# Expert layers of a fused network: gathered rows transposed two tiles ahead, result stores three tiles behind the loads of weight pieces

## The chip, the cores and the metric

The kernel runs as one program on one NeuronCore of a Trainium2 chip. Its time is the device time of one execution in microseconds; the figure compared is the median of several executions. Engines: TensorE (PE in the profile, with PEld for its weight loads), VectorE (DVE), ScalarE (ACT), GpSimd (POOL), SyncE (SP), and 16 DMA engines. All five work through their own instruction streams in order, and meet at semaphores.

## What is computed

The network has four layers: an adaptive convolution with a box convolution, a softmax attention with a mixture of experts, and a linear attention with a second mixture of experts. The change touches the two mixtures of experts alone. Of 4096 tokens of 128 channels each, every one goes to its 2 best of 8 experts:

```python
g = jnp.einsum('sd,edh->esh', flat, w_gate)
u = jnp.einsum('sd,edh->esh', flat, w_up)
y = jnp.einsum('esh,ehd->esd', silu(g) * u, w_down)
out = jnp.einsum('esd,se->sd', y, dense_w)      # dense_w: softmax over the two chosen
```

The hidden width is 256 in the first expert layer (names with `d_`) and 512 in the second (names with `f_`).

## The kernel before

Routing sorts the (token, expert) pairs into 71 tiles of 128 rows, each tile with one expert. `experts` is then called once for each layer, and goes over these 71 tiles. The order on each engine is written out by hand, and semaphores join the engines. For tile n:

- **GpSimd** gathers the tile's 128 rows from HBM into one of four buffers `xg` by an indirect DMA (`gather`), AHEAD = 3 tiles in front of its own loop; gather n waits until tile n-4 has been transposed. In the second layer it also writes the results by an indirect DMA (`scatter`).
- **TensorE** transposes the rows into PSUM (`transpose_x`), forms gate and up in three passes (`gate_up`: high x high, high x low, low x high parts of numbers split in two), transposes the hidden tile (`transpose_h`) and multiplies it by the expert's output weights (`down`). Before `transpose_x` it reads the number of the expert into a register (`load_expert`, a TENSOR_LOAD).
- **ScalarE** applies Silu to gate (`gate`), copies the transposed rows to SBUF as the high part (`copy_x`), and copies the transposed hidden tile (`copy_h`).
- **VectorE** subtracts to get the low part (`low_x`), multiplies up by Silu(gate) (`hidden`), and copies the result out of PSUM (`result`).
- **SyncE**, in the first layer, stores the result tile to HBM.

TensorE's loop body is the part that the change is about: `gate_up(n)`, `transpose_x(n+1)`, `transpose_h(n-1)`, `down(n-2)`. `gate_up(n+1)` waits for `low_x(n+1)`, which waits for `copy_x(n+1)`, which stands behind `gate(n)` on ScalarE, which waits for `gate_up(n)`.

The first layer also prepares the input weights of the second, in 16 pieces of 128x512 (256 KB), one in each of its first 16 tiles (`WeightSplit`, names `f_raw`, `f_w_high`, `f_w_low`). SyncE loads a piece into one of two buffers, ScalarE copies it as the high part at the end of its loop body (L1181), and VectorE subtracts for the low part at the end of its own (L1190). The load of piece n+2 waits for the low part of piece n. On SyncE it stands between the stores of result n-1 and n; result n-1 is made two loop bodies after its gate_up.

PSUM: in the first layer the transposed rows and the results have two banks each; in the second one each (`OWN = 1`), so that `transpose_x(n)` there waits for `low_x(n-1)`. The SBUF tiles of high and low parts have two buffers each in both layers.

Of the kernel before, what the change touches and what calls it, by code (L numbers as in the profile page):

```python
# [27 lines left out]
P = 128  # L28
# [34 lines left out]
class Kit:  # L63
# [7 lines left out]
    def sb(self, name, shape, dt=F32):  # L71
        return self.ctx.enter_context(self.nc.sbuf_tensor(name, shape, dt))

    def sem(self, name):
        s = self.ctx.enter_context(self.nc.semaphore(name))
        Kit.used.append(s)
        return s
# [1674 lines left out]
def experts(nc, top, moe, split=None):  # L1752
# [4 lines left out]
    ps, ident = top.ps, top.ident  # L1757
    F, TILES_IN = moe.F, moe.SLOT_TILES
    CHUNKS = F // P
    AHEAD = 3  # L1760
    RING = 8
    tag = moe.tag
    with ExitStack() as ctx:  # L1763
# [9 lines left out]
        y = sb("y", [P, RING, C])  # L1773
        gathered = sem(*(f"gathered{b}" for b in range(4)))
        stored = sem(*(f"stored{b}" for b in range(RING)))
        xT_ps, x_high_ready, x_ready, gu_ps, silu_ready, h_ready, h_ps, hT_ready, y_ps, y_ready = sem(
            "xT_ps", "x_high_rd", "x_rd", "gu_ps", "silu_rd", "h_rd", "h_ps", "hT_rd", "y_ps", "y_rd")
# [12 lines left out]
        if moe.by_slot:  # L1790
            @block.sync
            def _(sp):
                if split is not None:
                    for i in range(2):
                        split.load(sp, i)
                for n in range(TILES_IN):
                    if split is not None and n + 2 < split.pieces:
                        split.load(sp, n + 2)
                    sp.wait_ge(y_ready, n + 1)
                    sp.dma_start(moe.y_dram[n * P:(n + 1) * P, :], y[:, n % RING]).then_inc(stored[n % RING], 16)  # L1800
                for b in range(RING):
                    sp.wait_ge(stored[b], 16 * ((TILES_IN - b + RING - 1) // RING))

        @block.gpsimd
        def _(pool):
# [13 lines left out]

            for n in range(AHEAD):  # L1820
                gather(n)
            for n in range(TILES_IN):
                if n + AHEAD < TILES_IN:
                    gather(n + AHEAD)
                if not moe.by_slot and n >= 3:
# [7 lines left out]
        @block.tensor  # L1833
        def _(pe):
            keep_warm(nc, top, 3, 7)
            pe.wait_ge(moe.weights_in, 16)
            expert = [pe.alloc_register(f"{tag}_expert{b}") for b in range(4)]

            nc.disable_value_cache = True

            def of_expert(w, n):
                e = bass.RuntimeValue.of_register_unchecked(expert[n % 4]).with_bounds(min_val=0, max_val=moe.E - 1)
                return w[:, bass.ds(e, 1), :].rearrange("p e f -> p (e f)")

            def load_expert(n):
                pe.reg_load(expert[n % 4], moe.expert[0:1, n:n + 1])

            def transpose_x(n):
                pe.wait_ge(gathered[n % 4], 16 * (n // 4 + 1))
                if n >= OWN:  # L1850
                    pe.wait_ge(x_ready, n - OWN + 1)
                nc.tensor.transpose(XT(n), xg[:, n % 4, :], ident[:]).then_inc(xT_ps, 1)  # L1852

            def gate_up(n):
                pe.wait_ge(x_ready, n + 1)
                if n >= 2:
                    pe.wait_ge(h_ready, n - 1)
                passes = ((xT, moe.w_high), (xT, moe.w_low), (xT_low, moe.w_high))
                for i, (x, w) in enumerate(passes):
                    if wide:  # L1860
                        for o, cols in ((GATE(n), slice(0, F)), (UP(n), slice(F, 2 * F))):
                            ins = nc.tensor.matmul(o, x[:, n % 2, :], of_expert(w, n)[:, cols],  # L1862
                                                   start=(i == 0), stop=(i == len(passes) - 1))
                    else:
                        ins = nc.tensor.matmul(ps[:, n % 2, 0:2 * F], x[:, n % 2, :], of_expert(w, n),  # L1865
                                               start=(i == 0), stop=(i == len(passes) - 1))
                ins.then_inc(gu_ps, 1)

            def transpose_h(n):
                pe.wait_ge(h_ready, n + 1)  # L1870
                if n >= 2:
                    pe.wait_ge(hT_ready, n - 1)
                for c in range(CHUNKS):
                    ins = nc.tensor.transpose(HT(n)[:, c * P:(c + 1) * P], h[:, n % 2, c * P:(c + 1) * P], ident[:])
                ins.then_inc(h_ps, 1)

            def down(n):
                pe.wait_ge(hT_ready, n + 1)
                if n >= OWN:
                    pe.wait_ge(y_ready, n - OWN + 1)  # L1880
                for c in range(CHUNKS):
                    e = bass.RuntimeValue.of_register_unchecked(expert[n % 4]).with_bounds(min_val=0, max_val=moe.E - 1)
                    ins = nc.tensor.matmul(Y(n), hT[:, n % 2, c * P:(c + 1) * P],  # L1883
                                           moe.w_out[:, bass.ds(e, 1), c, :].rearrange("p e c -> p (e c)"),
                                           start=(c == 0), stop=(c == CHUNKS - 1))
                ins.then_inc(y_ps, 1)

            load_expert(0)
            transpose_x(0)
            for n in range(TILES_IN + 2):  # L1890
                if n < TILES_IN:
                    gate_up(n)
                if n + 1 < TILES_IN:
                    load_expert(n + 1)
                    transpose_x(n + 1)
                if 1 <= n <= TILES_IN:
                    transpose_h(n - 1)
                if n >= 2:
                    down(n - 2)
            nc.disable_value_cache = False  # L1900

        @block.scalar
        def _(act):
            def gate(n):
                act.wait_ge(gu_ps, n + 1)
                if n >= 2:
                    act.wait_ge(h_ready, n - 1)
                nc.scalar.activation(silu[:, n % 2, :], GATE(n), ACT.Silu).then_inc(silu_ready, 1)  # L1908

            def copy_x(n):  # L1910
                act.wait_ge(xT_ps, n + 1)
                if n >= 2:
                    act.wait_ge(gu_ps, n - 1)
                nc.scalar.activation(xT[:, n % 2, :], XT(n), ACT.Copy).then_inc(x_high_ready, 1)  # L1914

            def copy_h(n):
                act.wait_ge(h_ps, n + 1)
                if n >= 2:
                    act.wait_ge(y_ps, n - 1)
                nc.scalar.activation(hT[:, n % 2, :], HT(n), ACT.Copy).then_inc(hT_ready, 1)  # L1920

            copy_x(0)
            for n in range(TILES_IN + 1):
                if n < TILES_IN:
                    gate(n)
                if n + 1 < TILES_IN:
                    copy_x(n + 1)
                if n >= 1:
                    copy_h(n - 1)
                if split is not None and n < split.pieces:  # L1930
                    split.high_on_scalar(act, n)

        @block.vector
        def _(dve):
            def low_x(n):
                dve.wait_ge(x_high_ready, n + 1)
                nc.vector.tensor_tensor(xT_low[:, n % 2, :], XT(n), xT[:, n % 2, :], ALU.subtract).then_inc(x_ready, 1)  # L1937

            def hidden(n):
                dve.wait_ge(silu_ready, n + 1)  # L1940
                if n >= 2:
                    dve.wait_ge(h_ps, n - 1)
                nc.vector.tensor_tensor(h[:, n % 2, :], UP(n), silu[:, n % 2, :], ALU.mult).then_inc(h_ready, 1)  # L1943

            def result(n):
                dve.wait_ge(y_ps, n + 1)
                if n >= RING:
                    dve.wait_ge(stored[n % RING], 16 * (n // RING))
                nc.vector.tensor_copy(y[:, n % RING, :], Y(n)).then_inc(y_ready, 1)  # L1949

            low_x(0)
            for n in range(TILES_IN + 2):
                if n + 1 < TILES_IN:
                    low_x(n + 1)
                if n < TILES_IN:
                    hidden(n)
                if n >= 2:
                    result(n - 2)
                if split is not None and n < split.pieces:
                    split.low(dve, nc.vector, n)  # L1960
# [187 lines left out]
```

## Time and profile before

| | us |
|---|---|
| median of 3 executions | 969.69 (969.58 to 978.5) |
| the profiled execution | 975.88 |
| its span, first to last instruction | 974.1 |
| mean granted clock of TensorE | 0.871 of full speed |
| first expert layer's tiles, in the span | about 394 to 551 |
| second expert layer's tiles, in the span | about 729 to 943 |

Times of day below are microseconds from the start of the span. The granted clock is 1.00 at 2.4 GHz and 0.50 at 1.2 GHz. In the profile a matmul's duration includes the way through the array, so matmuls that follow each other overlap: the distance from start to start is what one costs. Float32 matmuls of `down` appear as two records each.

### The profile page before, as it was taken

The page shows a single profiled execution, that of the slowest core. Times are in us where ns is not written, and L with a number is a line of the kernel's source. Part 1 is how long each engine was busy: PE and PEld are TensorE (multiplying, and loading weights), DVE is VectorE, ACT ScalarE, POOL GpSimd, SP SyncE. Part 2 cuts the span into 40 slices and gives each one's busy share as a digit, 9 for nine tenths or more (in the row PEclk, how much of TensorE's full clock was granted, in tenths as well). Part 3 has the DMA queues.
Part 4 walks back from the last instruction along what each step waited for, and adds up shares of the span by engine and source line. Part 5 has one row for each costly group of instructions (what it writes and reads, how often), then busy time and mean ns, then how long its engine had stood idle before and what let it go on. Part 6 is the DMA issues. An engine that isn't in the chain of part 4 may idle for free. (4 is left out here: it accounts for less than half of the span.)

```text
span 974.1 us, 17847 instructions
## 1 busy us (share of the span) xinstructions
PE 746.4 (77%) x4853; PEld 590.5 (61%) x4853; DVE 544.4 (56%) x1589; ACT 456.9 (47%) x1147; POOL 437.2 (45%) x464
## 2 busy tenths in 40 slices
PE   3797978989998736769999535566479999999960
PEld 1575846666665535446666424554367888888850
DVE  6587946777775559354444255776573333333326
ACT  1994435767775314444444334552144444444424
POOL 5000444655652060434444277831015666666734
PEclk9899887999997755899999867987559999999995
DMA  2000000000000240452222211102201111111107
GB/s 97 1 0 19 3 1 2 2 0 0 0 1 2 77 140 1 119 147 64 66 66 66 54 49 50 49 16 76 98 8 34 44 44 47 42 47 41 50 19 259
DMA packets 34197, 46.24 MB, mean 47 GB/s; under 512 B 8227, under 2 KB 22887, under 8 KB 33872
## 3 DMA queue, kind: packets, MB, share of 16 engines
q1 hardware_dynamic: 25264, 27.66, 8.8%
q0 software_dynamic: 8864, 17.72, 6.9%
q8 instruction: 36, 0.59, 0.3%
q14 instruction: 33, 0.27, 0.1%
HBM read 30.21 MB, written 15.60 MB: 47 GB/s over the span
## 5 line engine op out<-in xcount | busy, mean ns | idle before, releaser
L1809 POOL DMA_INDIRECT d_xg<-d_normed,d_gather x71 | 68.3, 961 | 104.5 <-PE ps L1852 79.6
L1047 DVE TENSOR_REDUCE negmax<-ps 128x2 f32<-128x512 f32 x128 | 82.6, 688 | 51.9 <-PE ps L881 51.1
L1809 POOL DMA_INDIRECT f_xg<-f_normed,f_gather x71 | 69.0, 971 | 78.5 <-SPq L1763 55.0
L1908 ACT ACTIVATE f_silu<-ps 128x512 f32<-128x512 f32 x71 | 42.5, 598 | 118.9 <-PE ps L1862 118.9
L1937 DVE TENSOR_TENSOR f_x_low<-ps,f_x_high 128x128 fp32r<-128x128 f32 x71 | 20.7, 292 | 135.5 <-ACT f_x_high L1914 135.5
L1815 POOL DMA_INDIRECT f_results<-f_y,f_scatter x71 | 71.9, 1013 | 54.4 <-issue 39.3
L788 ACT ACTIVATE prob<-ps 128x512 f32<-128x512 f32 x128 | 69.6, 598 | 44.4 <-PE ps L900 44.4
L1261 POOL DMA_INDIRECT e_yg<-d_results,d_slot_u x64 | 61.0, 953 | 32.9 <-issue 18.2
L1883 PE MATMUL ps<-f_w_out,f_hT 128*128 x568 | 75.2, 275 | 0.7 <-DVE f_y L1949 0.7
L1883 PEld LDWEIGHTS ps<-f_w_out,f_hT 128*128 128x128 f32 x568 | 69.0, 192 | 0.9 <-issue 0.9
L1937 DVE TENSOR_TENSOR d_x_low<-ps,d_x_high 128x128 fp32r<-128x128 f32 x71 | 20.6, 290 | 73.6 <-ACT d_x_high L1914 73.6
L1908 ACT ACTIVATE d_silu<-ps 128x256 f32<-128x256 f32 x71 | 27.1, 382 | 67.5 <-PE ps L1865 67.5
L725 POOL TENSOR_SCALAR q_low<-q,lower 128x512 fp32r<-128x512 f32 x16 | 24.9, 1559 | 66.3 <-ACT q L768 45.5
L1865 PE MATMUL ps<-d_w_high,d_x_high 128*128 x71 | 35.7, 503 | 23.9 <-DVE d_x_low L1937 15.8
L1862 PE MATMUL ps<-f_w_high,f_x_high 128*128 x142 | 51.7, 445 | 2.7 <-DVE f_x_low L1937 2.7
L898 PE MATMUL ps<-qa,ka 32*128 32x256 f32 x256 | 42.7, 348 | 11.8 <-DVE qb L1053 8.9
L1345 PE MATMUL ps<-ident,e_xn 128*128 128x128 f32 x32 | 9.0, 374 | 55.0 <-ACT e_xn L1311 55.0
L1943 DVE TENSOR_TENSOR f_h<-ps,f_silu 128x512 f32<-128x512 f32 x71 | 48.3, 681 | 1.8 <-ACT f_silu L1908 1.7
L1883 PE MATMUL ps<-d_w_out,d_hT 128*128 x284 | 48.2, 292 | 0.1
L327 PE MATMUL ps<-fcol,wimg 128*128 (+1 forms) x160 | 41.0, 404 | 5.9 <-ACT wimg L283 5.5
L1862 PE MATMUL ps<-f_w_high,f_x_low 128*128 x142 | 44.8, 396 | 0.0
L1862 PE MATMUL ps<-f_w_low,f_x_high 128*128 x142 | 44.6, 395 | 0.0
(353 smaller groups left out, 2105.0 us busy)
## 6 DMA issues: line engine op xcount, KB each, us to landing
d_results<-d_y SPq DMA_DIRECT2D x71, 64.0 KB
f_raw<-in_f_in SPq DMA_DIRECT2D x16, 256.0 KB, 2.8
f_ys<-f_results SPq DMA_DIRECT2D x8, 512.0 KB, 7.3
X<-in_x SPq DMA_DIRECT2D x4, 512.0 KB, 5.5
d_normed<-X SPq DMA_DIRECT2D x8, 256.0 KB, 2.0
d_raw<-in_d_in SPq DMA_DIRECT2D x8, 256.0 KB, 2.8
f_normed<-X SPq DMA_DIRECT2D x8, 256.0 KB, 2.0
f_w_out<-in_f_out SPq DMA_DIRECT2D x1, 2048.0 KB, 8.2
```

Source lines behind the costliest of these rows:

```text
L327: last = nc.tensor.matmul(ps[:, 2 + b, a * PIX:(a + 1) * PIX], wimg[:, a, t, :], rhs.rearrange("p n r c -> p (n r) c"), start=(t == 0), st ...
L788: nc.scalar.activation(prob[:, h].rearrange("p t q -> p (t q)"), ps[:, h % 2, :], ACT.Exp, scale=SCALE).then_inc(prob_ready, 1)
L898: nc.tensor.matmul(o, ka[rows, b, g, keys], qa[rows, b, g, :], start=True, stop=False)
L1047: nc.vector.tensor_reduce(negmax[:, :, h // HG, col:col + 1], ps[:, 2 + h % 2, :].rearrange("p (t k) -> p t k", t=2), AX_X, ALU.max, negat ...
L1261: nc.gpsimd.indirect_dma_start(yg[:, n % 4, t, c, :], None, first.y_dram, bass.IndirectOffsetOnAxis(ap=first.slot[:, c, tile:tile + 1], ax ...
L1809: nc.gpsimd.indirect_dma_start(xg[:, n % 4, :], None, moe.xn_dram, bass.IndirectOffsetOnAxis(ap=moe.gather[:, n:n + 1], axis=0)).then_inc( ...
L1815: nc.gpsimd.indirect_dma_start(moe.y_dram, bass.IndirectOffsetOnAxis(ap=moe.scatter[:, n:n + 1], axis=0), y[:, n % RING, :], None, bounds_ ...
L1862: ins = nc.tensor.matmul(o, x[:, n % 2, :], of_expert(w, n)[:, cols], start=(i == 0), stop=(i == len(passes) - 1))
L1883: ins = nc.tensor.matmul(Y(n), hT[:, n % 2, c * P:(c + 1) * P], moe.w_out[:, bass.ds(e, 1), c, :].rearrange("p e c -> p (e c)"), start=(c ...
L1908: nc.scalar.activation(silu[:, n % 2, :], GATE(n), ACT.Silu).then_inc(silu_ready, 1)
L1937: nc.vector.tensor_tensor(xT_low[:, n % 2, :], XT(n), xT[:, n % 2, :], ALU.subtract).then_inc(x_ready, 1)
L1943: nc.vector.tensor_tensor(h[:, n % 2, :], UP(n), silu[:, n % 2, :], ALU.mult).then_inc(h_ready, 1)
```

## The change

Three orders are changed in `experts`, for both layers, and one on SyncE, for the first:

- `transpose_x`, `copy_x` and `low_x` run for tile n+2 where they ran for n+1. Two of each stand ahead of the loops. On VectorE `low_x` moves behind `hidden`.
- Gathers run 4 tiles ahead (AHEAD) instead of 3, still in four buffers.
- SyncE stores result n-3 in loop body n instead of result n; the loads of weight pieces keep their bodies.

```diff
-    AHEAD = 3
+    AHEAD = 4
...
-                for n in range(TILES_IN):
+
+                def store(n):
+                    sp.wait_ge(y_ready, n + 1)
+                    sp.dma_start(moe.y_dram[n * P:(n + 1) * P, :], y[:, n % RING]).then_inc(stored[n % RING], 16)
+
+                for n in range(TILES_IN + 3):
                     if split is not None and n + 2 < split.pieces:
                         split.load(sp, n + 2)
-                    sp.wait_ge(y_ready, n + 1)
-                    sp.dma_start(moe.y_dram[n * P:(n + 1) * P, :], y[:, n % RING]).then_inc(stored[n % RING], 16)
+                    if n >= 3:
+                        store(n - 3)
...
             load_expert(0)
-            transpose_x(0)
+            for n in range(2):
+                transpose_x(n)
             for n in range(TILES_IN + 2):
                 if n < TILES_IN:
                     gate_up(n)
                 if n + 1 < TILES_IN:
                     load_expert(n + 1)
-                    transpose_x(n + 1)
+                if n + 2 < TILES_IN:
+                    transpose_x(n + 2)
                 if 1 <= n <= TILES_IN:
                     transpose_h(n - 1)
                 if n >= 2:
...
-            copy_x(0)
+            for n in range(2):
+                copy_x(n)
             for n in range(TILES_IN + 1):
                 if n < TILES_IN:
                     gate(n)
-                if n + 1 < TILES_IN:
-                    copy_x(n + 1)
+                if n + 2 < TILES_IN:
+                    copy_x(n + 2)
...
-            low_x(0)
+            for n in range(2):
+                low_x(n)
             for n in range(TILES_IN + 2):
-                if n + 1 < TILES_IN:
-                    low_x(n + 1)
                 if n < TILES_IN:
                     hidden(n)
+                if n + 2 < TILES_IN:
+                    low_x(n + 2)
                 if n >= 2:
                     result(n - 2)
```

SyncE's stream at the start of the first expert layer, as a difference (- before, + after); f_raw is a weight piece, d_results a result tile:

```order
-L1177 DMA f_raw<-in_f_in 128x512 x3
-L1800 DMA d_results<-d_y 128x128
+L1177 DMA f_raw<-in_f_in 128x512 x6
+L1799 DMA d_results<-d_y 128x128
```

Six loads now stand ahead of the first store, where three did; each later load stands three stores further ahead.

VectorE's stream at the same place, before: d_x_low is `low_x`, d_h is `hidden`, f_w_low the low part of a weight piece.

```order
L1937 TENSOR_TENSOR d_x_low<-ps,d_x_high 128x128 x2
L1943 TENSOR_TENSOR d_h<-ps,d_silu 128x256
L1190 TENSOR_TENSOR f_w_low<-f_raw,f_w_high 128x512
L1937 TENSOR_TENSOR d_x_low<-ps,d_x_high 128x128
L1943 TENSOR_TENSOR d_h<-ps,d_silu 128x256
```

The same place after:

```order
L1945 TENSOR_TENSOR d_x_low<-ps,d_x_high 128x128 x2
L1951 TENSOR_TENSOR d_h<-ps,d_silu 128x256
L1945 TENSOR_TENSOR d_x_low<-ps,d_x_high 128x128
L1190 TENSOR_TENSOR f_w_low<-f_raw,f_w_high 128x512
L1951 TENSOR_TENSOR d_h<-ps,d_silu 128x256
```

The two ahead are now both in front of the loop, and each later `low_x` stands behind `hidden` of the same body.

ScalarE's first rows of the layer, before: d_x_high is `copy_x`, and the table load is that of Silu.

```order
L1914 ACTIVATE d_x_high<-ps 128x128
L1908 ACT_TABLE_LOAD
L1908 ACTIVATE d_silu<-ps 128x256
L1914 ACTIVATE d_x_high<-ps 128x128
L1181 ACTIVATE f_w_high<-f_raw 128x512
```

The same rows after:

```order
L1921 ACTIVATE d_x_high<-ps 128x128 x2
L1915 ACT_TABLE_LOAD
L1915 ACTIVATE d_silu<-ps 128x256
L1921 ACTIVATE d_x_high<-ps 128x128
L1181 ACTIVATE f_w_high<-f_raw 128x512
```

The table load and the first Silu now stand behind the copy of the second tile. Further on the streams read alike, one tile apart in what their rows work on.

## Rows read from the trace of the kernel before

**Rows 1.** Windows: each engine's busy us (x instructions), clock, DMA share, GB/s.

```profile
395.50:440.00 44.50, 30.92 (x160) 22.68 (x160) 22.99 (x64) 23.10 (x67) 17.38 (x18) 0.96 0.47 131
440.00:547.00 107.00, 97.43 (x531) 71.67 (x531) 43.64 (x160) 44.02 (x159) 46.70 (x50) 1.00 0.25 65
742.00:937.00 195.00, 195.00 (x1264) 174.33 (x1263) 72.86 (x201) 83.39 (x200) 129.41 (x131) 1.00 0.16 44
```

**Rows 2.** Waits in 386 to 552 us: who waited for whom, total us, times, longest.

```profile
ACT d_silu L1908 <- PE ps L1865: 67.5, 58, 1.5
```

**Rows 3.** Timeline of one first-layer tile: start us, us, engine, line, op, [idle before].

```profile
492.43 0.50 PE L1865 MATMUL ps<-d_w_high,d_x_high 128*128 x1
...
493.43 0.38 ACT L1908 ACTIVATE d_silu<-ps 128x256 f32<-128x256 f32 x1 [1.19 <-PE ps L1865]
...
493.60 0.69 PE L1883 MATMUL ps<-d_w_out,d_hT 128*128 x4
493.71 0.27 ACT L1914 ACTIVATE d_x_high<-ps 128x128 fp32r<-128x128 f32 x1
...
494.01 0.29 DVE L1937 TENSOR_TENSOR d_x_low<-ps,d_x_high 128x128 fp32r<-128x128 f32 x1 [1.20 <-ACT d_x_high L1914]
...
494.45 0.49 PE L1865 MATMUL ps<-d_w_high,d_x_high 128*128 x1 [0.16 <-issue]
```

**Rows 4.** Timeline of one second-layer tile.

```profile
802.74 0.27 PE L1852 MATMUL ps<-ident,f_xg 128*128 128x128 f32 x1
...
802.93 0.60 ACT L1908 ACTIVATE f_silu<-ps 128x512 f32<-128x512 f32 x1 [1.69 <-PE ps L1862]
...
803.28 1.06 PE L1883 MATMUL ps<-f_w_out,f_hT 128*128 x8
...
803.94 0.68 DVE L1943 TENSOR_TENSOR f_h<-ps,f_silu 128x512 f32<-128x512 f32 x1
...
804.17 0.73 PE L1862 MATMUL ps<-f_w_high,f_x_high 128*128 x2
...
805.67 0.27 PE L1852 MATMUL ps<-ident,f_xg 128*128 128x128 f32 x1
```

**Rows 5.** L1809, gathers of both layers: from issue to landing.

```profile
DMA to landing us min/median/max: 2.5/2.6/3.8
```

**Rows 6.** Timeline around one weight piece, from the store ahead to its use.

```profile
402.98 0.33 SPq L1800 DMA_DIRECT2D d_results<-d_y  x1
...
403.35 0.43 SPq L1177 DMA_DIRECT2D f_raw<-in_f_in  x1
...
406.11 0.63 ACT L1181 ACTIVATE f_w_high<-f_raw 128x512 fp32r<-128x512 f32 x1 [1.72 <-DMA f_raw<-in_f_in]
...
406.77 0.69 DVE L1190 TENSOR_TENSOR f_w_low<-f_raw,f_w_high 128x512 fp32r<-128x512 f32 x1 [1.80 <-ACT f_w_high L1181]
```

**Rows 7.** The tile f_raw, the raw weight pieces.

```profile
L1181 ACT ACTIVATE f_w_high<-f_raw x16: 622/630/642, 396.9 to 438.3; 128x512 fp32r<-128x512 f32 x16
...
DMA to landing us min/median/max: 2.7/2.8/3.1
```

**Rows 8.** Timeline of ScalarE where the weight pieces end.

```profile
438.87 0.39 ACT L1908 ACTIVATE d_silu<-ps 128x256 f32<-128x256 f32 x1
...
441.02 0.38 ACT L1908 ACTIVATE d_silu<-ps 128x256 f32<-128x256 f32 x1 [1.33 <-PE ps L1865]
```

**Rows 9.** Timeline of the first layer's start.

```profile
391.61 0.95 POOL L1809 DMA_INDIRECT d_xg<-d_normed,d_gather  x1 [0.30 <-issue]
...
395.05 1.28 ACT L1908 ACT_TABLE_LOAD   x1
...
396.51 0.38 ACT L1908 ACTIVATE d_silu<-ps 128x256 f32<-128x256 f32 x1 [0.17 <-PE ps L1865]
```

**Rows 10.** Timeline of TensorE at the second layer's start.

```profile
733.75 0.72 PE L1862 MATMUL ps<-f_w_high,f_x_high 128*128 x2 [1.16 <-DVE f_x_low L1937]
...
736.67 0.74 PE L1862 MATMUL ps<-f_w_high,f_x_high 128*128 x2 [0.72 <-DVE f_x_low L1937]
```

## The prediction

> **What bounds the kernel now.** I looked first at windows over the two places that the change touches. In the second expert layer TensorE is busy 195.00 of 195 us at clock 1.00; in the first it is busy 97.43 of 107 us once the weight pieces are done, and only 30.92 of 44.5 us while they last [rows 1]. So the second layer is bound by TensorE itself and can give back only what its start loses; the first has room. The waits of the first layer say why: ScalarE waited 67.5 us for gate_up before Silu, in 58 of 71 tiles [rows 2].
>
> The timeline of one tile shows the circle [rows 3]. gate_up starts at 492.43; Silu starts at 493.43, when it is done; the copy of the next tile's rows stands behind Silu, at 493.71; low_x follows at 494.01 and ends at 494.30; only then does the next gate_up start, at 494.45. That is 2.02 us a tile, though TensorE's fourth down matmul began about 0.4 us after 493.60 and nothing follows it. low_x(n+1) depends on transpose_x(n+1) alone by its data; only ScalarE's order ties it to gate_up(n).
>
> **Part 1: transposes two ahead, first layer, tiles after the weight pieces.** After the change gate_up(n+1) needs low_x(n+1) of one body earlier, ready about 2 us before it is asked for. The circle is then Silu, copy, low_x once in two tiles: 2.02 / 2 = 1.0 us a tile, and no longer the bound. What is late next? TensorE's own work. From gate_up's start to the first down matmul it is 1.17, over three gate_up passes and three transposes [rows 3]. Four down records cost 4 x 0.11 = 0.45 at the second layer's pace (0.89 us for eight, 803.28 to 804.17 [rows 4]), or about 0.55 as they stand in the first (0.69 for four, less the last one's 0.29, makes 0.13 to 0.14 between starts). So 1.62 to 1.72 a tile. A second way: 9.57 us idle over 53 tiles is 0.18 each [rows 1], and each gap hides behind a modelled matmul end of 0.29 where the next start could have come after 0.13: 0.18 + 0.16 = 0.34 to be had, 1.68. I take 1.66, in the middle.
>
> The others keep up with 1.66. ScalarE's three operations start 0.28, then 0.16 apart, and the last takes 0.39: 0.83. VectorE's three are of similar size, about 0.8. A gather is 0.95 plus 0.30 of issue, 1.25 [rows 9], and takes 2.6 us to land, 3.8 at worst [rows 5]. Its place: AHEAD grows with the transposes, so gather n still starts when transpose_x(n-4) is done and has four tiles, 6.6 us, before transpose_x(n) asks for it, which queues transpose_h and down behind it on TensorE. 0.3 + 3.8 = 4.1 fits into 6.6. Had AHEAD stayed 3 GpSimd would not wait for longer either, since nothing but gathers stands in its stream here. The stores move behind by three tiles, which ring buffer y (8) covers: VectorE's result(n) needs store n-8.
>
> Sum: 52 tiles (18 to 70) x (2.02 - 1.66) = **18.7 us**; with 1.72 it is 15.6, with 1.60 it is 21.8.
>
> **Part 2: the 16 tiles with weight pieces.** Now the load at 403.35 stands behind the store at 402.98, which waited for result 0, though its buffer had been free for two microseconds; the piece reaches ScalarE at 406.11, where the copy had waited 1.72 us and all of ScalarE's next body with it [rows 6]. High parts run from 396.9 to 438.3 in 15 steps, 2.76 us a tile [rows 7]. With the stores three behind, the result that a store waits for is always there (result n-3 is made in body n-1, low part n in body n), so a load waits only for the low part of the piece in its buffer. What is late next is that circle itself: high part to low part 0.66, low part 0.69, issue about 0.04, landing 2.76 here [rows 6] and 2.7 to 3.1 over all [rows 7]; with 2.9 it is 4.29 us for the two tiles between uses of a buffer, **2.15 a tile** instead of 2.76. This is above TensorE's 1.66 and above ScalarE's 0.83 + 0.63 = 1.46, so the loads stay the bound here, and part 1 alone would give nothing on top.
>
> The start costs something. copy_x(1) now stands ahead of Silu's table load (1.28 us), and needs the second gather, issued at 391.61 [rows 9]. With 3.7 to land (near the worst of [rows 5]) it arrives at 395.3, the copy is done at about 396.0, the table at 397.3: Silu(0) at 397.3 instead of 396.51 [rows 9], 0.8 later, and with it piece 0. If the gather lands in 2.6 this cost is gone. Then: low part 0 done at 399.1, piece 2 at ScalarE at 402.0, six turns of 4.29 to piece 14 at 427.7, piece 15 about 1.3 behind at 429.0, against 438.3. Silu(16) comes at 429.6 instead of 438.87, 9.3 us sooner. Before, Silu(17) came at 441.02 [rows 8] and Silu(18) one tile of 2.02 later, 443.04. After, TensorE has had both gate_ups ready or free to start, and Silu(18) comes at about 431.5: **11.5 us** saved up to there. With landings of 3.1 it is 10; with 2.7 and no loss at the start it is 13.5.
>
> The DMA engines are 0.47 busy at 131 GB/s while the pieces load [rows 1]. A piece and two row tiles in 2.15 us are 384 KB, about 183 GB/s, or 0.66 busy at the same price: room, but less of it. The Trainium skill ("DMA: Bandwidth & Descriptors", Latency and other measured facts) gives HBM's access latency as 0.2 us on average and 2 us at high load, which would speak against a landing as short as today's. By it a landing could grow by up to 1.8 us and the circle to 3.0 a tile, slower than before in this stretch by 4 us; no row here shows such a landing.
>
> **Part 3: the second layer.** TensorE starts a transpose of rows every 2.93 us (802.74, 805.67 [rows 4]), and its work is the same, so nothing changes in steady state. One bank holds the transposed rows here, so transpose_x(n+2) waits for low_x(n+1), which VectorE now makes behind hidden(n-1). Silu starts at 802.93, 1.70 after its gate_up (804.17 less 2.93); with Silu 0.60, hidden 0.68 [rows 4], low_x 0.29 as in the first layer and 0.1 of handing over, low_x ends 3.4 after gate_up(n-1), 0.5 after gate_up(n), and the transpose is asked for 1.5 after it: 1.0 us of slack. At the start TensorE waited 1.16 us before gate_up(1) and 0.72 before gate_up(2) [rows 10]; these 1.9 go. The table load behind copy_x(1), and transpose_x(1) waiting for low_x(0) ahead of gate_up(0), cost 0.2 to 0.4. Net **1.5 us**. The ends of both layers are as they were, and what follows moves with them.
>
> **Sum.** 18.7 + 11.5 + 1.5 = 31.7 us. The profiled execution of 975.88 would become 944.2. It is 6.2 us above the median of 969.69; I take the saving off the median as it is: **938 us**, 3.3% less.
>
> **Rivals.**
> 1. *TensorE's instruction supply sets the tile.* Each first-layer tile has a TENSOR_LOAD and five address instructions among its matmuls. If they run only at the pace seen after a release, a tile is 1.17 + 0.55, and 0.15 from the releasing low_x (494.30) to gate_up (494.45): 1.87 [rows 3]. Part 1 shrinks to 52 x 0.15 = 7.8, and the time is 949. For it: down starts 0.13 apart here against 0.11 there. Against: the second layer runs without a gap with ten address instructions and a TENSOR_LOAD in 2.93 us [rows 1, 4]. The Trainium skill ("DMA: Bandwidth & Descriptors", Latency and other measured facts) puts the floor of a tensor_load at about 600 ns, which speaks for this rival: by it one load a tile would leave 1.06 of 1.66 us for the other instructions. No row shows the register read by itself.
> 2. *The loads gain nothing*, because stores and gathers lengthen landings by as much as the queue loses: 2.76 a tile stays. Part 2 shrinks to the two tiles behind the pieces, about 2: 947.5. Against: landings were 2.7 to 3.1 with a store right ahead of each load.
> 3. *Steady tiles stay at 2.02*, because the new order closes another circle that I don't see: the wait moves and the time is 957. Against: no circle over two tiles that I can draw is longer than 1.46 a tile beside TensorE's.
> 4. *Slower: the single bank of the second layer.* If low_x(n+1) behind hidden(n-1) comes late, transpose_h and down queue behind a waiting transpose. Each 0.1 us past the 1.0 of slack costs 7.1 us over 71 tiles; from 0.45 us late, thus low_x 1.45 us later than I reckon, the change is a loss, and at 0.6 the time is 981. Silu and hidden would have to start far later than they do.
>
> **How the numbers follow.** Forecast 0.62 (own range 932 to 944); rival 1 0.14; rival 2 0.07; rival 3 0.06; rival 4 0.03; more gain than forecast, if tiles reach 1.55, 0.05; nothing gained at all 0.03. The range is 930 to 949.5. A measurement of this kernel can tell about 1% from no change. Faster by over 1% (below 960): 0.93. Within 1%: 0.04. Slower: 0.03.
>
> **What would show it.** In the profile after: Silu of the first layer 1.6 to 1.7 us apart behind the pieces, TensorE without idle time there, and ScalarE's 67.5 us of waits for gate_up still long but harmless; loads issued within 0.1 us of the low part and high parts 2.15 apart in pairs; the second layer's tiles still 2.93 apart. Wrong would be: waits of TensorE for gathers, landings well over 3.1, or a gap before each transpose of the second layer.

## The result: 4.8 to 5.6% faster, more than forecast

| | before | after | ratio, 95% interval |
|---|---|---|---|
| first measurement, median | 969.63 us (4 executions) | 917.47 us (4) | 0.9438 [0.9374, 0.9503] |
| measured again, median | 971.97 us (11) | 925.88 us (6) | 0.9525 [0.9488, 0.9562] |
| profiled execution, its span | 974.1 us | 918.5 us | |

Medians are over all executions; ratios and their intervals leave out those that took over 1.5% longer than the fastest of the same kernel.

The forecast was 938 us, in a range of 930 to 949.5. The time is below it. The profiles say where, in stretches between events that both traces have (first gather of the first layer, weight load of the linear attention, first gather of the second layer, load of the results for the last sum):

| stretch, us | before | before, second trace | after | after, second trace |
|---|---|---|---|---|
| up to the first expert layer | 390.1 | 380.4 | 381.5 | 384.8 |
| first expert layer | 162.8 | 162.4 | 125.2 | 125.3 |
| linear attention and routing | 173.2 | 172.1 | 171.8 | 172.9 |
| second expert layer | 224.1 | 225.3 | 216.3 | 215.0 |
| last sum | 23.9 | 23.9 | 23.7 | 23.8 |

The expert layers gave 37 and 8 to 10 us, 45 to 47 together. The stretch ahead of them, which nobody edited, takes 380 to 390 us; that is the likely reason why the first measurement shows 52 us.

The windows of the kernel after, behind the weight pieces and in the second layer, with the same columns as in [rows 1]; the first stretch is that with the pieces:

```profile
388.00:421.00 33.00, 27.16 (x158) 20.04 (x157) 21.75 (x61) 21.33 (x64) 17.06 (x18) 1.00 0.62 174
424.00:498.00 74.00, 74.00 (x498) 64.00 (x496) 40.44 (x148) 41.37 (x150) 44.33 (x47) 1.00 0.35 88
695.00:880.00 185.00, 185.00 (x1242) 164.48 (x1241) 71.55 (x195) 81.60 (x196) 126.71 (x128) 1.00 0.16 46
```

TensorE now shows 74.00 of 74 us in the first layer as well, where it showed 97.43 of 107 [rows 1]. The waits in the first layer, against [rows 2]:

```profile
ACT d_silu L1915 <- PE ps L1870: 35.5, 53, 0.8
...
ACT f_w_high L1181 <- DMA f_raw<-in_f_in: 11.7, 14, 1.8
...
PE ps L1879 <- DVE d_h L1951: 6.0, 11, 1.2
```

ScalarE waits for gate_up 35.5 us instead of 67.5, and behind the pieces this wait is now harmless: TensorE has no idle time there. TensorE waits 6.0 us for `hidden` in 11 waits, in tiles with pieces and at the end, since it shows no idle time from 424 to 498.

One tile of the first layer, as in [rows 3]:

```profile
442.40 0.48 PE L1870 MATMUL ps<-d_w_high,d_x_high 128*128 x1
...
442.67 0.28 DVE L1945 TENSOR_TENSOR d_x_low<-ps,d_x_high 128x128 fp32r<-128x128 f32 x1
...
443.39 0.38 ACT L1915 ACTIVATE d_silu<-ps 128x256 f32<-128x256 f32 x1 [0.65 <-PE ps L1870]
...
443.51 0.61 PE L1888 MATMUL ps<-d_w_out,d_hT 128*128 x4
...
443.88 0.48 PE L1870 MATMUL ps<-d_w_high,d_x_high 128*128 x1
```

A tile takes 1.48 us (442.40 to 443.88) instead of 2.02. `low_x` at 442.67 is for the next gate_up, at 443.88. It ends at 442.95, 0.93 before that gate_up starts, where the prediction reckoned with about 2 and the kernel before had 0.14 to 0.15.

One tile of the second layer, as in [rows 4]:

```profile
800.44 0.27 PE L1857 MATMUL ps<-ident,f_xg 128*128 128x128 f32 x1
...
800.99 1.06 PE L1888 MATMUL ps<-f_w_out,f_hT 128*128 x8
801.80 0.72 PE L1867 MATMUL ps<-f_w_high,f_x_high 128*128 x2
...
803.27 0.27 PE L1857 MATMUL ps<-ident,f_xg 128*128 128x128 f32 x1
```

A transpose of rows comes every 2.83 us (800.44 to 803.27) instead of every 2.93. Most of the tenth went ahead of gate_up: from the first down matmul to gate_up it is 0.81 (800.99 to 801.80), and it was 0.89 (803.28 to 804.17 [rows 4]).

The tile f_raw, as in [rows 7]:

```profile
L1181 ACT ACTIVATE f_w_high<-f_raw x16: 630/632/644, 388.7 to 420.5; 128x512 fp32r<-128x512 f32 x16
...
DMA to landing us min/median/max: 2.7/2.9/3.4
```

High parts are (420.5 - 388.7) / 15 = 2.12 us apart (2.17 in the second trace), with landings of 2.9 and at most 3.4.

### The profile page after: what moved, and what is told of

Read it like the earlier page. It is cut to its first block and busy times, and to the rows that moved or that the text cites. A ratio compares the mean times of both kernels' runs of the same rounds, so it can differ in the third digit from the quotient of the medians.

```text
span 918.5 us, 17847 instructions
## 1 busy us (share of the span) xinstructions
PE 709.9 (77%) x4853; PEld 570.1 (62%) x4853; DVE 548.4 (60%) x1589; ACT 456.9 (50%) x1147; POOL 436.2 (47%) x464
## 5 line engine op out<-in xcount | busy, mean ns | idle before, releaser
L1915 ACT ACTIVATE f_silu<-ps 128x512 f32<-128x512 f32 x71 | 42.4, 597 | 108.9 <-PE ps L1867 108.9
L1820 POOL DMA_INDIRECT f_results<-f_y,f_scatter x71 | 71.9, 1013 | 46.1 <-issue 34.5
L1261 POOL DMA_INDIRECT e_yg<-d_results,d_slot_u x64 | 60.9, 952 | 31.7 <-issue 18.2
L1951 DVE TENSOR_TENSOR d_h<-ps,d_silu 128x256 f32<-128x256 f32 x71 | 30.0, 423 | 37.6 <-ACT d_silu L1915 37.6
L1888 PE MATMUL ps<-d_w_out,d_hT 128*128 x284 | 44.8, 280 | 0.1
L1915 ACT ACTIVATE d_silu<-ps 128x256 f32<-128x256 f32 x71 | 27.0, 380 | 35.6 <-PE ps L1870 35.5
L1927 ACT ACTIVATE f_hT<-ps 128x512 f32<-128x512 f32 x71 | 42.9, 604 | 1.1 <-PE ps L1879 1.1
L898 PEld LDWEIGHTS ps<-qa,ka 32*128 32x128 f32 x256 | 25.2, 189 | 29.2 <-DVE negmax L1047 10.2
```

Source lines behind the costliest of these rows:

```text
L898: nc.tensor.matmul(o, ka[rows, b, g, keys], qa[rows, b, g, :], start=True, stop=False)
L1261: nc.gpsimd.indirect_dma_start(yg[:, n % 4, t, c, :], None, first.y_dram, bass.IndirectOffsetOnAxis(ap=first.slot[:, c, tile:tile + 1], ax ...
L1820: nc.gpsimd.indirect_dma_start(moe.y_dram, bass.IndirectOffsetOnAxis(ap=moe.scatter[:, n:n + 1], axis=0), y[:, n % RING, :], None, bounds_ ...
```

## The experiments

Each was profiled, so its stretches can be compared with the table above. "First" and "second" are the stretches of the two expert layers; the tiles behind the pieces are means from Silu(18) to Silu(70), those of the second layer from Silu(0) to Silu(70). The second mean holds a shorter start; in the middle of that layer a tile takes 2.94 us in the kernel before and 2.83 in the changed one. The runs were timed in three sets, each with the kernel before beside them: its median was 971.5 us beside the runs from null_before to ahead3, 969.1 beside copy_first, second_only, two_loads and the first raw3, and 972.0 beside the others. A ratio is to the one of its set.

| kernel | median us | ratio to before | first | high parts apart | tile behind them | second | tile |
|---|---|---|---|---|---|---|---|
| before | 971.5 | | 162.8 | 2.76 | 2.02 | 224.1 | 2.93 |
| changed | 925.9 | 0.953 | 125.2 | 2.12 | 1.50 | 216.3 | 2.81 |
| null_before | 972.4 | 1.002 [0.998, 1.007] | 162.4 | 2.71 | 2.02 | 225.3 | 2.94 |
| transposes_only | 937.7 | 0.967 [0.959, 0.975] | 134.2 | 2.75 | 1.50 | 216.3 | 2.81 |
| stores_only | 966.5 | | 154.3 | 2.19 | 2.02 | 225.3 | 2.94 |
| ahead3 | 922.4 | 0.955 [0.947, 0.963] | 125.8 | 2.18 | 1.50 | 216.4 | 2.82 |
| copy_first | 959.0 | 0.984 [0.975, 0.994] | 154.6 | 2.65 | 1.86 | 217.5 | 2.80 |
| second_only | 964.0 | 0.998 [0.993, 1.003] | 163.6 | 2.82 | 2.02 | 215.2 | 2.81 |
| two_loads | 943.5 | 0.971 [0.963, 0.979] | 146.1 | 2.23 | 1.88 | 216.3 | 2.81 |
| three_loads | 963.3 (one) | | 168.1 | 2.24 | 2.23 | 224.1 | 2.93 |
| no_load | 923.1 (one) | | 124.7 | 2.20 | 1.48 | 216.4 | 2.81 |
| raw3, twice | 916.2, 914.2 | 0.943, 0.938 [0.933, 0.942] | 117.8, 117.5 | 1.65, 1.63 | 1.50 | 216.3, 215.1 | 2.81 |

The executions of `stores_only` spread from 949.6 to 970.5 us, so it has no ratio and is read by its stretches.

### The kernel before once more (null_before)

No edit.

> The kernel before once more, unchanged, to see how far stages that nobody edited move between profiled executions. From the first instruction to the first gather of the first expert layer the trace of before took 390.1 us and that of the changed kernel 381.5. If that is a matter of the execution (TensorE's granted clock in the attention stage), this kernel's own stretch comes out anywhere from 381 to 391 us; if the edit of the expert layers did it (program length, code in another place), it stays within 1 us of 390. Expert layers: 162.8 us from the first gather to the weight load of the linear attention, tiles 2.02 apart; second layer 224.1 us, tiles 2.93 apart.

Its first stretch is 380.4 us, where the first trace of the same kernel took 390.1. The windows show the place; first the kernel before in its first trace, from 310 to 322 us, at the end of the softmax attention:

```profile
310.00:322.00 12.00, 10.84 (x77) 6.75 (x68) 2.08 (x6) 4.33 (x9) 0.00 (x0) 0.50 0.00 0
```

And in its second trace:

```profile
310.00:322.00 12.00, 6.49 (x59) 4.02 (x58) 3.32 (x12) 4.57 (x8) 0.87 (x7) 0.96 0.00 0
```

The granted clock was 0.50 here in one execution and 0.96 in the other, with unchanged code. Over the fourteen traces the router's load, behind this place, stands at 320 to 323 us in nine and at 327 to 329 in five, and the kernel before is in both groups. The stretch of linear attention and routing moves too, from 167 to 176 us. So two totals of the same kernel can differ by 7 us and more, and the 52 us of the first measurement may hold some of that; the repeated medians differ by 46.1 us, as the two expert layers' stretches do. One thing stays open: all eight traces of kernels with the whole change are among the nine early ones, and five of the six others are in the late group. `null_before` shows that no edit is needed to get from one to the other; whether the edit makes the early one more frequent isn't shown.

### The two parts apart (transposes_only, stores_only)

The first has the change without SyncE's part, the second SyncE's part alone:

```diff
 # transposes_only: SyncE keeps the order of before, everything else is the changed kernel
...
-                for n in range(TILES_IN + 3):
+                for n in range(TILES_IN):
                     if split is not None and n + 2 < split.pieces:
                         split.load(sp, n + 2)
-                    if n >= 3:
-                        store(n - 3)
+                    sp.wait_ge(y_ready, n + 1)
+                    sp.dma_start(moe.y_dram[n * P:(n + 1) * P, :], y[:, n % RING]).then_inc(stored[n % RING], 16)
```

> The changed kernel with SyncE's order of before: transposes two ahead, AHEAD 4, stores and loads of pieces in the old order. My account of the two parts: in the 16 tiles with weight pieces the store ahead of each load holds the load back, so high parts stay about 2.76 us apart (at least 2.6), and only the tiles behind them run at 1.48 to 1.50: first layer about 162.8 - 27 - 2 = 134 us, the whole about 8 us slower than the changed kernel. Rival: the two-ahead order alone frees the loads as well, because results come sooner; then high parts are 2.1 to 2.3 apart and the time is that of the changed kernel. Second layer 216 us either way.

> The kernel before with the stores of results three behind the loads of pieces, everything else as before. If the load's circle (two buffers, high part, low part, load) sets the tiles with pieces, high parts are 2.1 to 2.2 apart here too, as the circle of Silu, copy and low_x takes 2.02 and fits: first layer 162.8 - 9 = 154 us, tiles behind the pieces still 2.02, second layer still 224 us: 9 to 10 us less than before in all. If the circle of 2.02 and the load's circle add up in part, since the high part stands on ScalarE between two Silus, high parts are 2.3 to 2.6 apart and the gain is 3 to 7 us.

The first layer takes 134.2 us with the transposes alone, 154.3 with the stores alone, 125.2 with both: 28.6, 8.5 and 37.6 us less than before. The parts add up (28.6 + 8.5 = 37.1), since each has its own tiles. With the old store order the load still stands behind its store; SyncE in `transposes_only`:

```profile
408.24 0.33 SPq L1800 DMA_DIRECT2D d_results<-d_y  x1
408.61 0.43 SPq L1177 DMA_DIRECT2D f_raw<-in_f_in  x1
410.46 0.33 SPq L1800 DMA_DIRECT2D d_results<-d_y  x1
410.83 0.43 SPq L1177 DMA_DIRECT2D f_raw<-in_f_in  x1
```

The tile f_raw there, and then in `stores_only`:

```profile
L1181 ACT ACTIVATE f_w_high<-f_raw x16: 629/631/656, 396.1 to 437.3; 128x512 fp32r<-128x512 f32 x16
...
DMA to landing us min/median/max: 2.7/3.0/3.2
```

```profile
L1181 ACT ACTIVATE f_w_high<-f_raw x16: 632/633/644, 396.6 to 429.5; 128x512 fp32r<-128x512 f32 x16
...
DMA to landing us min/median/max: 2.8/3.0/3.2
```

2.75 us between high parts in the one, 2.19 in the other, at the same landing of 3.0. The store ahead of the load was what held the pieces back: with the transposes alone they gain nothing, and with the stores alone nearly all (2.19, where both changes together give 2.12 to 2.17).

### AHEAD back at 3 (ahead3)

```diff
-    AHEAD = 4
+    AHEAD = 3
```

> The changed kernel with AHEAD at 3: gathers one loop body later beside the scatters of the second layer, no difference in the first layer, where GpSimd's stream holds gathers alone. If the gain of the second layer (224.1 to 216.3 us) came from TensorE's circle through low_x, this kernel keeps it: 216 to 217 us, 2.83 a tile, and the total is that of the changed kernel within 1 us; a gather still lands about 1 us before its transpose. Rival: the gathers' lead gave the second layer its gain; then this kernel goes back to 2.93 or above, 7 us or more slower, with TensorE waiting for f_xg.

The stretches are 125.8 and 216.4 us, as in the changed kernel. In the middle of the second layer a tile takes 2.85 us instead of 2.83, so the fourth gather ahead is worth about 1 us. The gain of the second layer isn't the gathers'.

### The circle shortened another way (copy_first)

The kernel before, with one swap on ScalarE:

```diff
-                if n < TILES_IN:
-                    gate(n)
                 if n + 1 < TILES_IN:
                     copy_x(n + 1)
+                if n < TILES_IN:
+                    gate(n)
```

> The kernel before, transposes one ahead as ever, with one swap on ScalarE alone: copy_x(n+1) stands ahead of gate(n) (Silu) instead of behind it. It shortens the circle gate_up, Silu, copy_x, low_x without touching TensorE's order, GpSimd or SyncE. My theory is that this circle set the pace of both layers before, the second one too, by 0.1 us a tile (low_x ended at 804.02, gate_up started at 804.17), although TensorE showed 195.00 of 195 us busy. Then the second layer falls from 2.93 to 2.81 to 2.83 a tile and from 224 to about 216 us. In the first layer copy_x starts at the end of the transpose (493.52 + 0.05), low_x ends at 494.15, gate_up starts 0.15 later: 1.87 a tile instead of 2.02, about 8 us less. Rival: the second layer was TensorE's own and its gain came from the new order on TensorE or GpSimd; then it stays at 2.93 here.

The second layer fell from 2.93 to 2.80 a tile with TensorE's stream untouched; in its middle a tile takes 2.83, as in the changed kernel. TensorE there, in its old order:

```profile
790.96 0.72 PE L1862 MATMUL ps<-f_w_high,f_x_high 128*128 x2
...
792.98 1.06 PE L1883 MATMUL ps<-f_w_out,f_hT 128*128 x8
793.79 0.48 PE L1862 MATMUL ps<-f_w_high,f_x_high 128*128 x1
```

From the first down matmul to gate_up it is 0.81 as in the changed kernel. VectorE at the same place:

```profile
793.06 0.29 DVE L1937 TENSOR_TENSOR f_x_low<-ps,f_x_high 128x128 fp32r<-128x128 f32 x1 [1.46 <-ACT f_x_high L1914]
```

`low_x` ends at 793.35, 0.44 before gate_up at 793.79, so gate_up no longer waits for it. In the kernel before it ended at 804.02:

```profile
803.73 0.29 DVE L1937 TENSOR_TENSOR f_x_low<-ps,f_x_high 128x128 fp32r<-128x128 f32 x1 [1.85 <-ACT f_x_high L1914]
```

and gate_up started at 804.17 [rows 4], 0.15 later, the same distance as from `low_x` (494.30) to gate_up (494.45) in the first layer [rows 3], where the wait was plain. This holds for every tile: over 45 tiles in the middle of the second layer gate_up starts 0.146 to 0.147 us behind the end of the last `low_x` in the kernel before, and 0.446 to 0.447 in `copy_first`. In the first layer the swap brought 2.02 to 1.86, where 1.87 was expected; there `low_x` still ends 0.14 ahead of gate_up, so the shortened circle still sets the tile.

### The second layer alone (second_only)

The changed kernel with `D = 1 if moe.by_slot else 2` for the depth, and the old stores: the first layer is that of before.

> The first layer exactly as before (one ahead, old stores), the second with transposes two ahead and AHEAD 4. First layer 162.5 us with 2.03 behind the pieces; second layer 216.3 us, 2.81 a tile, as in the changed kernel. Total about 8 us below the kernel before. If anything of the second layer's gain needs the first layer's change (its weights' parts written sooner, another clock), the second layer stays above 220 us.

215.2 us in the second layer and 163.6 in the first, so the two stretches together fell by 8.1 us. The ratio shows less of it than that, 0.998, and its interval, 0.993 to 1.003, leaves out the 0.992 that 8.1 us would be. The unedited stretches, which move by as much, are the likely reason; nothing here shows it.

### TensorE's instruction supply (two_loads, three_loads, no_load)

```diff
             def load_expert(n):
+                pe.reg_load(spare[n % 4], moe.expert[0:1, n:n + 1])
                 pe.reg_load(expert[n % 4], moe.expert[0:1, n:n + 1])
```

`down` then takes its expert from `spare`. `three_loads` has a third one for gate_up's last pass. `no_load` reads the number for the first four tiles only:

```diff
-                pe.reg_load(expert[n % 4], moe.expert[0:1, n:n + 1])
+                if n < 4:
+                    pe.reg_load(expert[n % 4], moe.expert[0:1, n:n + 1])
```

> The changed kernel with the register read of the expert's number done twice a tile (one register for gate_up, one for down). A test of the rival that TensorE's instruction supply sets the tile: if one such read cost about 0.6 us of it, two would need 1.2 of 1.48 us and the tile would go to 1.9 or more in the first layer. If supply runs ahead of the array, the first layer's tile stays at 1.48 to 1.55 and the second's at 2.81. A read of 0.1 to 0.3 us that is not hidden would show as 1.6 to 1.8.

> The changed kernel with three register reads of the expert's number a tile (gate_up's first two passes, its third pass, down). With two the first layer's tile went from 1.48 to 1.87: TensorE's instruction supply then sets the pace. The step from two to three gives the price of one read where supply sets the pace. If the step is 0.39, the kernel with one read was just at the point where supply takes over (1.48). If it is 0.5 to 0.7, the supply with one read needs 1.2 to 1.35 a tile and the array's 1.48 covers it: tiles at 2.4 to 2.55. The second layer has 2.81 a tile and should stay there with three reads, or rise to at most 3.0.

> The changed kernel with the expert's number read only for the first four tiles of each layer; later tiles use the weights of those four experts, so the choice of the expert is left out and the rest of the work is the same. If the array sets the changed kernel's tile, the first layer stays at 1.47 to 1.50 behind the pieces and the second at 2.81. If the register read is what is left on the path, tiles fall by the price of one read, to 1.1 or where GpSimd's gathers (1.25 a tile) end it.

The trace has the read as a row of its own, which the prediction said it hadn't; in the kernel before, on the sequencer of TensorE's weight loads (duration in ns, least, median and most):

```profile
L1846 PEldq TENSOR_LOAD <-d_expert x71: 295/301/495, 389.4 to 545.2; - x71
```

It takes 0.30 us, and the same in every other trace.

With two reads the first layer's tile goes from 1.50 to 1.88, with three to 2.23, without one to 1.48. The timeline of `two_loads` shows the stall behind the third pass of gate_up:

```profile
455.87 0.48 PE L1872 MATMUL ps<-d_w_high,d_x_high 128*128 x1
...
456.42 0.39 PE L1872 MATMUL ps<-d_w_high,d_x_low 128*128 x1
...
456.84 0.14 PEld L1859 LDWEIGHTS ps<-ident,d_xg 128*128 128x128 f32 x1 [0.46 <-issue]
...
456.87 0.30 PE L1859 MATMUL ps<-ident,d_xg 128*128 128x128 f32 x1
...
457.77 0.48 PE L1872 MATMUL ps<-d_w_high,d_x_high 128*128 x1
```

The engine of the weight loads sits idle for 0.46 us ahead of the transpose's, put down as "issue" (it waited for nothing that the profile shows), and the transpose follows the third pass by 0.45 instead of 0.23. In `no_load` TensorE runs as in the changed kernel:

```profile
460.56 0.48 PE L1871 MATMUL ps<-d_w_high,d_x_high 128*128 x1
...
461.35 0.27 PE L1858 MATMUL ps<-ident,d_xg 128*128 128x128 f32 x1
...
461.67 0.61 PE L1889 MATMUL ps<-d_w_out,d_hT 128*128 x4
462.04 0.48 PE L1871 MATMUL ps<-d_w_high,d_x_high 128*128 x1
```

1.48 from gate_up to gate_up, and 0.37 from the first down matmul to gate_up. So the array sets 1.48, one read adds 0.02, the second 0.38 and the third 0.35. The second layer holds 2.81 with two and goes to 2.93 with three. The changed kernel stands right at the edge: by these steps instruction supply takes an estimated 1.88 - 0.35 to 0.38 = 1.50 to 1.53 us with one read, and the tile was 1.50. The Trainium skill ("DMA: Bandwidth & Descriptors", Latency and other measured facts) gives about 600 ns as a tensor_load's floor. The trace doesn't agree: a read takes 0.30 us here, and an added one costs 0.35 to 0.38.

### A version that beats both (raw3, raw3_again, after_again)

The changed kernel with three buffers for raw pieces:

```diff
-        self.raw = k.sb(f"{moe.tag}_raw", [P, 2, self.WIDTH])
+        self.raw = k.sb(f"{moe.tag}_raw", [P, self.BUFS, self.WIDTH])    # BUFS = 3
...
-        if i >= 2:
-            sp.wait_ge(self.low_ready, i - 1)
+        if i >= self.BUFS:
+            sp.wait_ge(self.low_ready, i - self.BUFS + 1)
```

> The changed kernel with three buffers for raw weight pieces instead of two. The load's circle of about 4.3 us (high part 0.66, low part 0.69, issue 0.04, landing 2.9) then spans three tiles, 1.43 a tile, less than ScalarE's own body with a high part (seen 1.57 us apart where a piece was there at once). So high parts 1.55 to 1.65 apart instead of 2.12, first layer 125.2 - 15 x 0.52 = about 117.5 us. Transfers then run at 384 KB in 1.6 us, 245 GB/s, near the 259 GB/s of the last stage; if landings lengthen to 3.5 and more, high parts are 1.7 to 1.9 apart and the gain is 3 to 6 us.

> The changed kernel once more, beside the next one. From the stages of seven traces: first expert layer 125 to 126 us, second 216.3, together 45 to 46 less than before; the rest moves by several us from execution to execution on its own (first stretch 380 to 391 in kernels that do not differ there), so the total is 45 to 46 us below before within what that noise allows: ratio 0.945 to 0.96.

> Three buffers for raw pieces, once more, timed on the same chip as the changed kernel: 7 to 8 us less than that one, all of it in the first expert layer (117.8 against 125.2 us).

High parts are 1.65 us apart, the first layer takes 117.8 and 117.5 us, 7.5 less than the changed kernel. The medians on one chip were 914.2 and 925.9 us; of those 11.7 us the traces explain 7.5 to 8, and the rest is within what the unedited stretches move by. The windows and the tile of `raw3`:

```profile
395.00:410.00 15.00, 14.59 (x92) 11.41 (x91) 12.48 (x36) 11.83 (x36) 9.09 (x10) 1.00 0.83 229
```

```profile
L1182 ACT ACTIVATE f_w_high<-f_raw x16: 624/631/653, 386.6 to 411.3; 128x512 fp32r<-128x512 f32 x16
...
DMA to landing us min/median/max: 2.7/3.4/4.6
```

The DMA engines are 0.83 busy at 229 GB/s, and the median landing grew from 2.9 to 3.4, at worst 4.6. The third buffer covers most of it: ScalarE waits 3.3 us in all for pieces, where it waited 11.7 in the changed kernel.

## Why the prediction was wrong

**The mechanism was right, two terms were too small.** Forecast and measured, in us saved in the traces:

| term | forecast | measured | how |
|---|---|---|---|
| first layer up to Silu(18) | 11.5 | 10.5 | 443.03 - 390.1 = 52.9 before, 423.94 - 381.5 = 42.4 after, from the first gather |
| 52 tiles behind it | 18.7 | 27.1 | 2.017 - 1.496 a tile |
| second layer | 1.5 | 7.8 to 10.3 | stretches above; 9.0 from Silu(0) to Silu(70) in both pairs of traces |
| sum | 31.7 | 45 to 47 | |

The lines of Silu(16) and Silu(18) after:

```profile
421.08 0.37 ACT L1915 ACTIVATE d_silu<-ps 128x256 f32<-128x256 f32 x1
...
422.01 0.38 ACT L1915 ACTIVATE d_silu<-ps 128x256 f32<-128x256 f32 x1
...
423.94 0.38 ACT L1915 ACTIVATE d_silu<-ps 128x256 f32<-128x256 f32 x1 [0.79 <-PE ps L1870]
```

**Part 1, 1.66 a tile, failed by 0.16.** The step that failed is the price of TensorE's own work: 1.17 from gate_up's start to the first down matmul, and 0.45 to 0.55 for four downs. Measured it is 1.11 and 0.37, together 1.48 (442.40, 443.51, 443.88). The downs were 0.12 too dear. The 0.89 for eight of them ended at a gate_up that waited for low_x, as `copy_first` shows (0.81 without the wait). And a gate_up that waits for nothing is recorded as starting 0.03 us behind the last down, not 0.11 or more; its own first pass is 0.32 long from start to start where the next is 0.23, so this 0.09 had been counted there and again among the downs. The other 0.06 are in the 1.17, which was read behind a gate_up that had just been released: its transposes are 0.13 apart, those of the changed kernel 0.11. The second way, from the windows, gave 1.68 by the same habit: it let the next start come 0.13 behind the last down. That two ways agreed meant little, because both took a start that had been waited for as the end of work.

**Part 3, "the second layer is TensorE's own", was false.** This is the step that cost most for its size: the sum had nothing for the steady tiles, and 0.10 us each over 71 tiles is 7. The start, for which it had 1.5, gave 2.0 by itself (Silu(0) to Silu(2) takes 3.85 us instead of 5.86). 195.00 of 195 us busy and a start every 2.93 us looked like a bound. The circle gate_up, Silu, copy_x, low_x ran there too and set 2.93; TensorE's work was 2.83, the tile that `copy_first`, `second_only`, `two_loads` and `no_load` all have in the middle of the layer. The 0.1 us of wait hid under the modelled end of the last down matmul, so the view of busy time was full and the view of waits empty. The trace of before had it: `low_x` ends at 804.02 and gate_up starts at 804.17, the same 0.15 as in the first layer. I never put the two side by side, since a full windows row had told me that there was nothing to look for.

**Part 2 held, but for its end.** The load's circle was forecast at 2.15 a tile and came out at 2.12 to 2.17, and no landing was over 3.6 in either trace. The start cost less than I feared: the second gather landed 2.4 us after its issue, not 3.7, and Silu(0) came 6.8 us after the first gather (388.3 - 381.5) where it took 6.4 before. Silu(16) came 39.6 us after the first gather, where 39.5 was forecast. The missing 1 us lies behind it: Silu(18) was to follow 1.9 us later and took 2.86 (421.08 to 423.94). On TensorE transpose_h stands ahead of that gate_up and waited for `hidden`, which VectorE made behind the low part of the last piece.

**The rivals.** Instruction supply (rival 1, 949) is a real limit, but not at its price: with one read it binds at about 1.50, the changed kernel's own pace, and not at 1.87, which takes a second read. Loads that gain nothing (rival 2) and tiles that stay at 2.02 (rival 3) did not come about; `transposes_only` shows what rival 2 would have looked like, 2.75. For the slower case (rival 4), the single bank of the second layer, no wait of a transpose for low_x is left in steady state: low_x ends at 799.33 in that trace, 1.1 us before the transpose at 800.44, where a slack of 1.0 was forecast. "More gain than forecast" was given 0.05, on tiles of 1.55; it is what happened.

**The noise.** The median of before was taken as firm because two of its three executions agreed within 0.1 us. Ten more of the same kernel spread from 965.1 to 978.0, and their mean granted clock from 0.879 at 965.1 to 0.863 at 978.0; two traces of it differ by the clock at the end of the attention. The 6 us between the first measurement's gain and the repeated one are of that size. What decides which clock an execution gets there stays open.

## What to carry to other kernels

An engine that is busy all the time in the profile may still be waiting, if waits are shorter than the part of a matmul's duration that overlaps the next: test it by the distance from the end of what releases it to its start, and compare that with a place where the wait is plain. When work is priced for a state without waits, take each distance from start to start where neither start waited, and count every boundary once. A transfer that refills a buffer should stand in its queue ahead of whatever waits for a later result; here moving the stores on SyncE was worth 8.5 us by itself.

## What the hardware showed that I had not expected

A register read of 0.30 us in TensorE's stream cost 0.02 us a tile or nothing while the array had a backlog (first layer with one read, second layer with one or two), and 0.35 to 0.38 us each once it had not. A tile of the changed kernel's first layer stands at that point: 1.48 without a read, 1.50 with one, 1.88 with two. And the same code found TensorE's granted clock at 0.50 in one execution and 0.96 in another at the same place, where the router's load then stood 7.5 us apart (328.5 and 321.0).
